# Dispatch of a soft mixture of experts: the cut of the running maxima spread over four units, and the token sums copied out bank by bank

## The reference, cut to what matters

```python
def _L0_ffn_ref(x, phi_w, phi_b, expert_w, expert_b):
    logits = (jnp.einsum('tzd,ed->tze', x, phi_w) + phi_b).reshape(t, z, n, p)
    D = jax.nn.softmax(logits, axis=3)
    C = jax.nn.softmax(logits, axis=2)
    X_tilde = jnp.einsum('tznp,tzd->npd', D, x)
    ...
    X_tilde = jnp.tanh(X_tilde)
    Y_tilde = jnp.einsum('npd,ndH->npH', X_tilde, expert_w) + expert_b[:, None, :]
    Y = jnp.einsum('tznp,npH->tzH', C, Y_tilde)
    return Y

x = x + _L0_attn_a_ref(_layernorm(x), ...)
x = x + _L0_ffn_ref(_layernorm(x), ...)
x = x + _L0_attn_b_ref(_layernorm(x), ...)
x = x + _L0_ffn_ref(_layernorm(x), ...)
```

## Time and profile before

| what | value |
|---|---|
| median of three executions | 4833.46 us (4826.34 to 4834.67) |
| the profiled execution | 4824.78 us, span 4823.1 us |
| TensorE busy over the span | 4443.6 us (92%) |
| VectorE busy | 4083.8 us (85%) |
| ScalarE busy | 3125.9 us (65%) |
| GpSimd busy | 1217.1 us (25%) |
| first dispatch | from 1626 us to 2011 us of the span |
| second dispatch | from 4006 us to 4393 us of the span |

### The profile page before, as it was taken

One profiled execution on the slowest core, in us unless ns is written; L12 is line 12 of the kernel. 1 busy time (PEld: TensorE's weight loads), 2 busy tenths in 40 slices (PEclk: granted clock), 3 DMA queues, 4 the chain that ended last, 5 costly groups with the idle time before them and its releaser, 6 DMA issues. The chain is left out here.

```text
span 4823.1 us, 97729 instructions
## 1 busy us (share of the span) xinstructions
PE 4443.6 (92%) x40558; PEld 1963.1 (41%) x40558; DVE 4083.8 (85%) x4665; ACT 3125.9 (65%) x5863; POOL 1217.1 (25%) x1201
## 2 busy tenths in 40 slices
PE   5789999999999799899987999999999998998998
PEld 3322223322223565556652222232222345664666
DVE  5699998999985898678847999989998868885887
ACT  2377898888998344334334789888899974443443
POOL 2000001100001577545401000011000015774543
PEclk9899999999999899999988999999999999999999
DMA  4200000000000000210031000000000000004000
GB/s 153 76 20 8 2 15 15 9 15 8 2 2 23 1 1 1 84 58 0 0 84 63 20 3 2 15 15 14 15 3 2 2 22 1 1 1 141 10 13 13
DMA packets 73656, 112.31 MB, mean 23 GB/s; under 512 B 12389, under 2 KB 56677, under 8 KB 68965
## 3 DMA queue, kind: packets, MB, share of 16 engines
q1 hardware_dynamic: 68634, 99.95, 6.2%
q0 software_dynamic: 4608, 6.50, 0.9%
HBM read 73.70 MB, written 31.47 MB: 22 GB/s over the span
## 5 line engine op out<-in xcount | busy, mean ns | idle before, releaser
L837 DVE TENSOR_REDUCE b_att_mx<-ps 128x2 f32<-128x1024 f32 (+3 forms) x1152 | 1227.8, 1129 | 103.4 <-PE ps L690 77.9
L837 DVE TENSOR_REDUCE a_att_mx<-ps 128x2 f32<-128x1024 f32 (+3 forms) x1152 | 1227.7, 1129 | 103.0 <-PE ps L690 77.5
L794 ACT ACTIVATE a_att_pt<-ps 128x512 f32<-128x512 f32 (+3 forms) x2304 | 1147.1, 560 | 207.2 <-PE ps L726 177.3
L794 ACT ACTIVATE b_att_pt<-ps 128x512 f32<-128x512 f32 (+3 forms) x2304 | 1146.8, 560 | 205.6 <-PE ps L726 176.4
L745 PE MATMUL ps<-b_att_pt,b_v 128*17 128x256 f32 (+1 forms) x8704 | 670.0, 380 | 10.6 <-ACT b_att_osb L781 9.8
L745 PE MATMUL ps<-a_att_pt,a_v 128*17 128x256 f32 (+1 forms) x8704 | 669.8, 380 | 10.8 <-ACT a_att_osb L781 9.8
L671 POOL TENSOR_SCALAR_AFFINE_SELECT a_att_pt<-a_att_pt 128x512 f32<-128x512 f32 x128 | 81.6, 637 | 1119.6 <-ACT a_att_pt L794 1107.3
L671 POOL TENSOR_SCALAR_AFFINE_SELECT b_att_pt<-b_att_pt 128x512 f32<-128x512 f32 x128 | 81.6, 637 | 1119.0 <-ACT b_att_pt L794 1106.7
L726 PE MATMUL ps<-a_q,a_k 51*128 51x512 f16 (+3 forms) x1152 | 360.8, 367 | 0.3 <-ACT a_att_pt L794 0.2
L726 PE MATMUL ps<-b_q,b_k 51*128 51x512 f16 (+3 forms) x1152 | 360.7, 367 | 0.2 <-ACT b_att_pt L794 0.2
L726 PE MATMUL ps<-a_att_q,a_att_k 51*128 51x512 f16 (+3 forms) x1152 | 338.6, 365 | 1.0 <-ACT a_att_pt L794 0.6
(11 more groups left out here) (319 smaller groups left out, 7258.2 us busy)
## 6 DMA issues: line engine op xcount, KB each, us to landing
f_mix_ct<-in_expert_w SPq DMA_DIRECT2D x64, 256.0 KB, 4.0
g_mix_ct<-in_expert_w SPq DMA_DIRECT2D x64, 256.0 KB, 4.1
a_parts_q<-a_qkv_cut SPq DMA_DIRECT2D x24, 256.0 KB, 2.8
a_parts_k<-a_qkv_cut SPq DMA_DIRECT2D x24, 256.0 KB, 2.8
b_parts_q<-b_qkv_cut SPq DMA_DIRECT2D x24, 256.0 KB, 2.9
b_parts_k<-b_qkv_cut SPq DMA_DIRECT2D x24, 256.0 KB, 2.8
x<-in_x SPq DMA_DIRECT2D x1, 4096.0 KB, 21.7
out<-x SPq DMA_DIRECT2D x8, 512.0 KB, 2.9
```

Source lines behind the costliest of these rows:

```text
L794: act.activation(pt[:, s % PT_RING, i, 0:width], ps[:, at:at + width], ACT.Exp, scale=unscale).then_inc(pt_ready, 1)
L837: dve.tensor_reduce(mx[u % 2][:, h:h + 2, t, c], both, AX.X, ALU.max).then_inc(ring_read, 1)
```

## The change

Three things change. The four operations of the cut are no longer issued together between d and lo of the unit that completes eight tiles. They are issued one per unit, each behind the unit's own lo: for the first cut behind lo(39), lo(40), lo(41) and lo(42). For the last cut all four stand behind lo(63). GpSimd's wait for its own last cut operation goes. The positions of T and of the copy of mct move three units back, to 45, 53 and 61; the last one stays at 66. And the copies of the four banks of sums wait for each bank by itself (xa_bank) instead of for the whole P; TensorE signals each bank after the last matmul that writes it.

```diff
-    TURN_AFTER = {min(n + 3, UNITS_D - 1 + LAG): j for n, j in CUT_AFTER.items()}
+    PIECES = 4
+    TURN_AFTER = {min(n + PIECES + 2, UNITS_D - 1 + LAG): j for n, j in CUT_AFTER.items()}
+    PIECE_AFTER = {n: [] for n in range(UNITS_D)}
+    for last_tile, j in CUT_AFTER.items():
+        for piece in range(PIECES):
+            PIECE_AFTER[min(last_tile + piece, UNITS_D - 1)].append((j, piece))
...
+                    if t == T - 1 and eb % 2 == 1 and eb + 1 < HALF_EB:
+                        mm.then_inc(xa_bank, 1)
                 mm.then_inc(xa_ready, 1)
...
-                    act.wait_ge(xa_ready, n - LAG + 1)
                     for b in range(HALF_EB // 2):
+                        if b + 1 < HALF_EB // 2:
+                            act.wait_ge(xa_bank, (HALF_EB // 2 - 1) * half + b + 1)
+                        else:
+                            act.wait_ge(xa_ready, n - LAG + 1)
...
-                pool.wait_ge(c_cut, j + 1)
...
-                if n in CUT_AFTER:
-                    cut_maxima(CUT_AFTER[n])
                 pool.wait_ge(high, n + 1)
                 pool.tensor_tensor(disp[:, n % DISP, 1, :], ex[:, n % EX, :], disp[:, n % DISP, 0, :],
                                    ALU.subtract).then_inc(d_ready, 1)
+                for j, piece in PIECE_AFTER[n]:
+                    cut_piece(j, piece)
```

More of the change, by code:

```diff
@@ L1020, in dispatch @@
         d_ready = sem("d_ready")
-        xa_ready = sem("xa_ready")
+        xa_ready, xa_bank = sem("xa_ready"), sem("xa_bank")
         xa_kept = sem("xa_kept")
@@ L1115, in _, with cut_piece @@
         def _(pool):
-            def cut_maxima(j):
+            def cut_piece(j, piece):
                 parts = m3[j % 2]
[L1119 to L1127, removed]
-                pool.wait_ge(c_cut, j + 1)
+                if piece == 0:
+                    pool.wait_ge(mc_made, j + 1)
+                    wait(pool, c_turned, j - 1)
+                    pool.tensor_copy(parts[:, :, 0, :], mc[:, :, :]).then_inc(c_chain, 1)
+                elif piece == 1:
+                    pool.wait_ge(c_chain, 3 * j + 1)
+                    pool.tensor_tensor(mrest[:, :, :], mc[:, :, :], parts[:, :, 0, :], ALU.subtract).then_inc(c_chain, 1)
+                elif piece == 2:
+                    pool.wait_ge(c_chain, 3 * j + 2)
+                    pool.tensor_copy(parts[:, :, 1, :], mrest[:, :, :]).then_inc(c_chain, 1)
+                else:
+                    pool.wait_ge(c_chain, 3 * j + 3)
+                    pool.tensor_tensor(parts[:, :, 2, :], mrest[:, :, :], parts[:, :, 1, :], ALU.subtract).then_inc(c_cut, 1)
             for n in range(UNITS_D):
```

## The result

The changed kernel took 4815.16 us (median of seven executions, 4811.94 to 4819.49), against 4829.56 us for the kernel before, of which seven were run by then (4824.22 to 4834.67). The ratio is 0.9970, with a 95% interval of 0.9961 to 0.9980: faster by 9.7 to 18.8 us. A second series of both kernels (the first experiment) gave 0.9976 (0.9965 to 0.9986). The direction was right, and the size was less than half of the 14.4 us between the medians. The profiled execution of the changed kernel took 4819.41 us, one of its two slowest.

What follows compares the result with a forecast made beforehand. A ring of three units paces the second half, no engine full. Cuts -0.46, lo(63) -1.18 and banks -1.42 us make -3.06 us per dispatch, -6.1 us for two: 4833.46 becomes 4827.4 us, range 4818 to 4841 us.

Steps and rivals of the forecast that it cites:

- What bounds the stage: Second half: no engine is full, a ring of three units sets the pace; the maxima cost 3.9 us per eight units.
- the wait before L(44) turned into one before L(47): On TensorE, L(44)'s 0.67 us wait for the copy of mct returns as 1.29 us before L(47), 0.80 us late.
- a shorter wait of d(46): Sign of being right: the 2.13 us that d(46) waits behind mc shrinks.
- The length of mc: On VectorE, mc's 1.82 us is a wait for lo and some 0.3 us of work; eight units take 46.63 us.
- Rival 1: mc has a fixed length, so 0.80 us stay per cut: -0.4 us, 4833.1 us; chance 0.20.
- The two terms of the tail: Dispatch end: lo(63) no longer behind four operations, -1.18 us; bank-by-bank copies beside P(63), -1.42 us.
- Rival 4: Bank signals bring nothing at the end, T or copy of mct late otherwise: +2.8 us, 4830.2 us; chance 0.10.
- the cost of a piece: On GpSimd, pieces take 0.48, 0.73, 0.48 and 0.75 us, 2.44 us in all, eating only the head start made.
- TensorE's clock: Falls of the clock in the second half: no saving summed; the third stretch, 47.69 us at 0.93, saves 0.18 us.
- rival 3: Fewer or shorter gaps keep TensorE at 2.4 GHz, 4825.6 to 4823.8 us, or slow other stretches, 4831.1 us; chance 0.17.
- ends for the three: Line for cuts 1 to 3: -3.9 us from the 1.23 us per cut gained, and +2.4 us, 0.80 each.
- Rival 2: GpSimd becomes the bound in the four units with pieces, 2.44 us bare: +6.9 us, 4840.4 us; chance 0.08.

Runs made afterwards that it cites:

- e8: e7 with ScalarE's copies of the first half's sums also moved in front of exp(34), with bank-by-bank waits: 4797.75 us, ratio 0.9932 to the kernel before.
- e5: The kernel before with only T and the copy of mct three units later (45, 53, 61): 4829.42 us, ratio 1.0002.
- e11: The changed kernel with only the copies of the first half's sums moved in front of exp(34): 4809.61 us, ratio 0.9956 to the kernel before.
- e7: The changed kernel with mc issued behind sum(n-1) and rec(n-1) on VectorE: 4809.94 us, ratio 0.9956 to the kernel before.
- e9: e8 with the cut and T put back as in the kernel before: 4800.27 us, ratio 0.9934 to the kernel before.
- e4: The changed kernel with the single wait for xa_ready put back, so pieces and T alone: 4825.45 us, ratio 0.9989 to the kernel before.
- e3: The kernel before with the bank signals and ScalarE's bank-by-bank waits alone: 4824.24 us, ratio 0.9987.
- e2: The kernel before with TensorE's new bank signals and nobody waiting for them: 4829.43 us, ratio 0.9994.
- e1: The changed kernel run again, unchanged, in a second series: 4817.98 us, ratio 0.9976 to the kernel before.
- e6: The changed kernel with its four pieces together behind lo(39), lo(47), lo(55) and T at 42, 50, 58: 4825.49 us, ratio 0.9990 to the kernel before.

## Why the prediction was wrong in its size, and what of it held

**What bounds the stage, and the course of each step: right.** lo(39), P(39) and L(43) early, the pieces eating the head start, the wait before L(44) turned into one before L(47), and the end of the first half without effect, all stand in the trace of the changed kernel. One sign that it named, a shorter wait of d(46), did not come, and did not follow from its own steps.

**The length of mc: right.** Where a lo runs beside it, it ends 0.27 to 0.28 us behind that lo, however long it is: 0.74 us (the first mc in e8), 1.14, 1.67 (e5), 1.82 and 2.26 us (the first mc in e11). With no lo beside it, or only one that ends 0.04 us after it starts, it is 0.36 us long (e7, e9). Rival 1 is out. The runs show that it waits for a GpSimd operation on the same SBUF; that it is a lock on a port, as the Trainium skill ("SBUF — State Buffer", SBUF: two separate sides) has it, fits each of these lengths, and no run here showed the port itself.

**The two terms of the tail: right.** -1.18 us forecast for lo(63) and 1.16 us measured (e4); -1.42 us forecast for the banks and 1.45 us measured (e3). Rival 4 is out. Together -5.3 us of the gain.

**The step that was mis-sized: the cost of a piece.** The forecast charged 0.48, 0.73, 0.48 and 0.75 us, the distances in a chain where each operation waits for the last. Behind a piece now stands an unrelated d, and the distances are 0.36, 0.62, 0.36 and 0.62 us: 1.96 us instead of 2.44 us. Only the first two pieces reach the length of the stretch. By them d(41) came 11.39 us behind d(39) and not 11.63 us (1869.06 in the forecast), and with it lo(41), P(41), for which TensorE waited 0.45 us, L(45), sub(45), L(46), sum(45) and lo(45). L(46) came at 25.66 us and not at 25.89 us (1883.32). So a stretch took 46.40 us and not 46.63 us. That is six times 0.23 us, 1.4 us in all. All four pieces together brought d(44), the copy of mct and L(47) 0.5 us earlier than forecast, but L(47) leads to sub(47) and mc, and mc waits for lo(45) in any case.

**The step that failed: TensorE's clock.** The sum put the falls of the clock at nothing: it took the third stretch's 47.69 us, let it come out alike with a saving of 0.18 us, and doubled the first dispatch for both. It gave the clock to rival 3, with 0.10 on the fast side. It was that rival which happened, in the stretches. In the profiles of before, e2 and e3, P(46) and P(54) waited 2.00 us, and in 11 of 12 cases that P took 4.46 us instead of 2.79 us and the stretch took 47.7 us. In the changed kernel, e1 and e4 they waited 1.3 us, and in none of 12 cases was it slow. A slow one costs 0.93 us. The profile that the forecast was made from has three slow ones in six stretches, worth 2.8 us; rival 3 counted one per dispatch, 1.8 us, with rows of the first dispatch alone, and the second has two. Over the three kernels that share its order here it is 11 of 18, so about 3.7 of 6, worth 3.4 us. In the tails rival 3's further gain did not come: P(61) runs at full speed in the changed kernel (4.06 us before), but that costs no time there, and P(62) is slow in both.

The length of the gap alone doesn't decide. Before P(38), in the first place of each dispatch, the same 2.00 us stood in nine kernels, and the P behind it was at full speed in all of their 18 cases but e11's second dispatch. In e6 all six gaps (before P(38), P(46) and P(54)) were 2.00 us and none of these P was slow. Behind the 1.85 us of e5, none of four was. What TensorE did before the gap is not the same in these cases, and no run takes the two apart. So it is shown that the falls went and what they cost, and it stays open why a gap brings one.

**The sum.** Six stretches by 0.37 us are 2.2 us, the falls of the clock 3.4 us, the tails 5.3 us: -10.9 us. In the forecast these terms were 0.9, 0 and 5.2 us. (Its line "ends for the three", -3.9 and +2.4 us, enters no total; together they would be -1.5 us and not the -0.46 us that it added.) The wholes in the table say much the same: a mean of 387.46 us for before and e2 against 382.33 us for changed and e1, 5.13 us per dispatch, 10.3 us in all. Both intervals of the ratio contain it (-18.8 to -9.7 us and -16.9 to -6.8 us). The medians' -14.4 and -12.2 us lie 2 to 4 us beyond. e2 excludes a gain from a new build larger than some 7 us, no more. Outside the two dispatches the profiles show no gain: the span less the two wholes is 4049.4 us for before, and 4051.9 and 4054.1 us for changed and e1. It goes from 4047.9 us (e3) to 4059.4 us (e2) over all 13 profiles, without an order by kernel. So these 2 to 4 us are of the size of the scatter, which one profile per kernel can't reduce.

**The baseline.** The forecast was an absolute time on a median of three executions, 4833.46 us. With four more the kernel before has 4829.56 us, and with other series 4829 to 4830 us. The missed 2.8 us are less than that shift of 3.9 us. The range counted the spread of the medians for only 2 to 3 us. A gain of more than 0.2%, which is what came, had a chance of 0.17 in the forecast.

**Rival 2** (pieces bare on GpSimd) was rightly held unlikely for the spread pieces, and e6 shows its price when they are not spread and T stands at 42: 1.5 us per stretch.

## What to carry to other kernels

A piece of side work is priced by what stands next to it. The same four operations cost 1.2 us inside a wait, 1.96 us spread between unrelated work and 2.3 us bare in a row. Wait that an operation spends inside its own duration is invisible as idle time: here an operation of a quarter of the size that took longer than its neighbour was such a wait, and moving it behind the work that others wait for gained 4.4 us per dispatch more (a mean whole of 377.94 us in e7 against 382.33 us), nearly as much as the change itself (5.13 us). Before a signal is made finer, one looks whether the waiting engine is there in time: here P(32) waited 3.8 us for ScalarE, and moving the copies in its order gained about 5 us per dispatch, the finer signal nothing at that place. At the end of the dispatch, where ScalarE was waiting for P(63), the same signal gained 1.45 us.

## What the runs showed of the hardware that I had not expected

- The GpSimd operations of 256 elements stand 0.11 to 0.12 us closer to the next operation when that one doesn't wait for their result (0.36 and 0.62 us against 0.48 and 0.73 us, start to start). e6 has both in one row: 0.48, 0.73 and 0.48 us, and 0.63 us to the unrelated d.
- A P behind a gap of 2.00 us ran in large part at 1.2 GHz (4.46 us instead of 2.79 us) in 11 of 12 cases, at P(46) and P(54) of one order of work, and in none of the four at the same places in another (e6); behind 1.85 us it did in none of four, behind 1.3 us in none of 12. When T alone was moved, the falls behind mc went and one came at P(63) (e5).
- A VectorE operation of 256 elements took anything from 0.36 to 2.26 us, and where it took longer than 0.36 us it ended 0.28 us behind the GpSimd operation that was running when it started.
- The falls of the clock repeat in a place more than I expected: in before, the changed kernel, e3 and e5 the tails of the two dispatches (13.01, 10.38, 11.56 and 14.67 us) agree to 0.01 us, with a slow P(62) in each. It is not a rule: in e7 the slow one is P(62) in the first dispatch and P(63) in the second, and the tails are 10.39 and 12.04 us.
